# A selective state-space scan: reading the states under C by turning them, instead of multiplying by broadcast rows

## The reference, cut to what matters

```python
x_dbl = einsum('bld,ed->ble', x, Wx)           # dt_rank 64 | B 16 | C 16
dt = softplus(x_dbl[..., :64] @ Wdt.T + bdt)
dA  = exp(dt[..., None] * A)                   # A = -exp(A_log), 512 x 16
dBx = (dt * x)[..., None] * Bm[:, :, None, :]
def step(hc, inp):                             # over the tokens of a sequence
    hc = dA_t * hc + dBx_t
    return hc, einsum('bdn,bn->bd', hc, C_t)
y = ys + x * Dp
y = y * silu(z)
out = einsum('bld,ed->ble', y, W_out)
```

## Time and profile before

| | before |
|---|---|
| median of 3 runs | 4064.31 us |
| profiled execution | 4061.75 us |
| its span, first to last instruction | 4059.8 us |
| mean granted TensorE clock over the span | 0.932 |
| DVE busy / PE busy / ACT busy / POOL busy | 2756.5 / 3550.4 / 1951.2 / 1562.0 us |

### The profile page before, as it was taken

The page is one execution under the profiler, slowest core; times in us unless marked ns, Lnnn a source line. Parts: engine busy times, 40 slices in busy tenths (PEclk is TensorE's granted clock), DMA queues, the critical chain, the costliest instruction groups (busy, mean ns, idle before and its releaser), DMA issues. The chain is left out here.

```text
span 4059.8 us, 128360 instructions
## 1 busy us (share of the span) xinstructions
PE 3550.4 (87%) x53914; PEld 2521.8 (62%) x53915; DVE 2756.5 (68%) x4627; ACT 1951.2 (48%) x3015; POOL 1562.0 (38%) x1491
## 2 busy tenths in 40 slices
PE   6999999999783699669999999998788888877778
PEld 4888888888672466448888888885233333333357
DVE  5777777777543122257777777776799999999964
ACT  2666666666441122126666666664444444444432
POOL 3333333333132100233333333330088777778800
PEclk8999999999895899869999999998898989999889
DMA  2010010000006100110100010000132222222200
GB/s 67 28 36 28 28 34 29 28 28 20 10 1 244 46 31 31 49 56 28 36 28 28 30 33 28 28 20 25 24 81 71 72 70 68 70 72 81 72 25 21
DMA packets 79948, 182.69 MB, mean 45 GB/s; under 512 B 10754, under 2 KB 31266, under 8 KB 79042
## 3 DMA queue, kind: packets, MB, share of 16 engines
q1 hardware_dynamic: 76354, 166.57, 13.2%
q0 software_dynamic: 3072, 8.39, 0.6%
HBM read 157.36 MB, written 17.56 MB: 43 GB/s over the span
## 5 line engine op out<-in xcount | busy, mean ns | idle before, releaser
L654 ACT ACTIVATE x_probs<-x_score_ps 128x1024 f32<-128x1024 f32 (+1 forms) x896 | 814.2, 960 | 708.2 <-PE x_score_ps L563 701.9
L714 DVE TENSOR_REDUCE x_maxes<-x_misc_ps 128x1 f32<-128x512 f32 (+1 forms) x1792 | 1020.9, 625 | 31.0 <-PE x_misc_ps L481 25.6
L678 POOL CAST x_kT_hi<-x_kT 128x512 fp32r<-128x512 f32 (+1 forms) x448 | 256.3, 572 | 1286.5 <-ACT x_kT L627 1063.1
L1742 PE MATMUL b_acc_ps<-b_read,ident 128*128 128x512 f32 x1024 | 571.1, 689 | 183.5 <-POOL b_read L1828 150.3
L1820 POOL TENSOR_TENSOR b_drive<-b_b_all,b_dtx 128x1024 f32<-128x1024 f32 x256 | 602.6, 2355 | 332.8 <-DVE b_dtx L1900 282.0
L1862 DVE TENSOR_TENSOR_SCAN b_state<-b_decay_ps,b_drive 128x512 f32<-128x512 f32 x512 | 607.0, 1205 | 12.5 <-POOL b_drive L1820 12.5
L557 PE MATMUL x_score_ps<-x_qz,x_kT 32*128 32x128 f32 x13312 | 591.2, 277 | 1.4 <-issue 1.2
L1810 ACT ACTIVATE b_decay_ps<-b_dt,b_a_neg 128x504 f32<-128x504 f32 x512 | 350.0, 685 | 462.3 <-DVE b_state L1862 462.3
L1742 PEld LDWEIGHTS b_acc_ps<-b_read,ident 128*128 128x128 f32 x1024 | 196.1, 213 | 503.8 <-POOL b_read L1828 251.1
L557 PEld LDWEIGHTS x_score_ps<-x_qz,x_kT 32*128 32x128 f32 x13312 | 501.4, 182 | 4.5 <-issue 2.5
L531 PE MATMUL x_misc_ps<-x_probs,x_v 128*32 128x64 f32 x26624 | 464.5, 221 | 0.0
(11 more groups left out here) (283 smaller groups left out, 5607.9 us busy)
## 6 DMA issues: line engine op xcount, KB each, us to landing
x_raw<-in_ctxT SPq DMA_DIRECT2D x64, 800.5 KB, 4.5
b_b_all<-b_bc_rows SPq DMA_DIRECT2D x128, 256.0 KB, 3.6
b_c_all<-b_bc_rows SPq DMA_DIRECT2D x128, 256.0 KB, 3.1
m_w<-in_m_w SPq DMA_DIRECT2D x16, 704.0 KB, 19.3
m_w<-in_m_w SPq DMA_DIRECT2D x8, 768.0 KB, 20.3
m_slot_rows<-m_zero SPq DMA_DIRECT2D x1, 4992.0 KB, 17.2
m_block_rows<-m_slot_rows SPq DMA_DIRECT2D x39, 128.0 KB, 2.0
m_slot_out<-m_out SPq DMA_DIRECT2D x39, 128.0 KB, 1.7
```

The lines of the kernel that those rows point to most:

```text
L654: nc.scalar.activation(probs[rows, s % 2, js, 0:n], score_ps[rows, js, 0:n], ACT.Exp).then_inc(exp_done, 1)
L678: nc.gpsimd.tensor_copy(kT_hi[:, at % 3, 0:m * even].rearrange("p (c k) -> p c k", c=m)[:, :, 0:kn], kT[:, b % 2, c:c + m, k0:k0 + kn]).th ...
L714: nc.vector.tensor_reduce(maxes[:, c:c + m, j, k0 // NB], bank(op)[:, 0:m * even].rearrange("p (c k) -> p c k", c=m)[:, :, 0:kn], AX.X, AL ...
L1742: nc.tensor.matmul(acc_ps[:, c, :], ident[:, :], read[:, c, :], start=False, stop=True, skip_group_check=True).then_inc(acc_done, 1)
```

## The change

The broadcast of C over the partitions is gone, and so are the three VectorE reads and the GpSimd read of a state. Instead the state is turned so that tokens lie on the partitions, where C_n(token) is a single number for each partition. There are TPB = 4 token tiles of 128 in a block. For every state TensorE transposes each token tile (four 128 x 128 transposes, one for each channel chunk) into one of two PSUM banks. ScalarE copies token tiles 0 to 2 out with C as its per-partition scale, and TensorE turns these back and adds them to acc_ps with four products per tile, in which the copied tile is the weights and the identity is what is streamed. Token tile 3 is summed over the 16 states in turned form by VectorE (`sum_tile`), and is turned back once, at the end of the pass. State and drive get two buffers. C itself is turned once, at the start of the first pass. In `project` the high and low parts, their buffers and their DMAs go. VectorE waits for the last gather of the whole pass before it takes the first chunk of acc_ps.

```diff
-                    sp.dma_start(bc_rows[d, :, tokens], xdbl[R:, d, tokens]).then_inc(rows_out, 16)
-                    for i, part in enumerate((hi, lo)):
-                        sp.dma_start(c_rows[d, i, :, tokens], part[R + NS:, d, :].bitcast(F32)).then_inc(rows_out, 16)
-                    sp.wait_ge(rows_out, blk * (2 * 48) + (d + 1) * 48)
-                    sp.sem_inc(rows_free, 1)
+                    sp.dma_start(b_rows[d, :, tokens], xdbl[R:R + NS, d, tokens]).then_inc(rows_out, 16)
+            sp.wait_ge(rows_out, NBLK * 2 * 16)
...
-                    nc.scalar.activation(xdbl[:, d, ds(blk * NB, NB)], dbl_ps[:, d, :], ACT.Copy)
-                    act.wait_ge(rows_free, blk * 2 + d + 1)
-                    nc.scalar.activation(hi[R:, d, :], dbl_ps[R:, d, :], ACT.Copy).then_inc(hi_done, 1)
+                    nc.scalar.activation(xdbl[:, d, ds(blk * NB, NB)], dbl_ps[:, d, :], ACT.Copy).then_inc(rows_done, 1)
...
-                low_parts(blk - 1)
-            low_parts(NBLK - 1)
...
+    BY_ACT = TPB - 1
+    PARTS = NS * BY_ACT + 1
+    drive = sb("b_drive", [P, 2, CI, NB])
+    state = sb("b_state", [P, 2, CI, NB])
+    read = sb("b_read", [P, BY_ACT, DI])
+    total = sb("b_total", [P, DI])
...
 @block.tensor
+        def turn_rows():                       # after the first Wdt products, pass 0 only
+            own = slice(R, R + 2 * NS)
+            for d in range(2):
+                for t in range(NT):
+                    ins = nc.tensor.transpose(turn_ps[:, d, t * 2 * NS:(t + 1) * 2 * NS], xdbl[own, d, t * P:(t + 1) * P],
+                                              ident[own, own])
+            ins.then_inc(rows_turned, 1)
+        def turn(k, i):
+            if i == 0:
+                pe.wait_ge(state_done, (k + 1) * CI)
+            if i >= 2:
+                pe.wait_ge(read_done, k * BY_ACT + i - 1)
+            elif k > 0 and i == 0:
+                pe.wait_ge(read_done, k * BY_ACT)
+            elif k > 0:
+                pe.wait_ge(total_done, k)
+            for c in range(CI):
+                ins = nc.tensor.transpose(turn_ps[:, i % 2, c * P:(c + 1) * P], state[:, k % 2, c, i * P:(i + 1) * P],
+                                          ident[:, :])
+            ins.then_inc(turn_done, 1)
+        def add_up(i, part):
+            for c in range(CI):
+                ins = nc.tensor.matmul(acc_ps[:, c, i * P:(i + 1) * P], part[:, c * P:(c + 1) * P], ident[:, :],
+                                       start=False, stop=True, skip_group_check=True)
+            ins.then_inc(acc_done, 1)
+        def gather(k, i):
+            pe.wait_ge(read_done, k * BY_ACT + i + 1)
+            add_up(i, read[:, i, :])
...
-                if n < NS - 1:
-                    make_c(k + 1)
-                for c in range(CI):
-                    gather(k, c)
+                turn(k, 0)
+                turn(k, 1)
+                if n > 0:
+                    gather(k - 1, 2)
+                turn(k, 2)
+                gather(k, 0)
+                turn(k, 3)
+                gather(k, 1)
+            gather((p + 1) * NS - 1, 2)
+            pe.wait_ge(total_done, (p + 1) * NS)
+            add_up(BY_ACT, total)
...
 @block.scalar
+        def read_tile(p, n, i):
+            k = p * NS + n
+            act.wait_ge(turn_done, k * TPB + i + 1)
+            if k > 0:
+                act.wait_ge(acc_done, p * PARTS + (n - 1) * BY_ACT + i + 1 if n > 0 else p * PARTS)
+            nc.scalar.activation(read[:, i, :], turn_ps[:, i % 2, :], ACT.Copy, scale=c_of(p, n, i)).then_inc(read_done, 1)
...
             for n in range(NS):
                 for c in range(CI):
+                    make_decay(p, n, c)
+                    if n > 0 and c > 0:
+                        read_tile(p, n - 1, c - 1)
+            for i in range(BY_ACT):
+                read_tile(p, NS - 1, i)
...
 @block.gpsimd
-            if k > 0:
-                pool.wait_ge(state_done, (k - 1) * CI + c + 2)
+            if k > 1:
+                pool.wait_ge(state_done, (k - 2) * CI + c + 2)
-                if n > 0:
-                    read_last(k - 1)
-            read_last(p * NS + NS - 1)
...
 @block.vector
+        def sum_tile(p, n):
+            dve.wait_ge(turn_done, (k + 1) * TPB)
+            if n == 0:
+                ins = nc.vector.tensor_scalar(total[:, :], tile, c_of(p, n, BY_ACT), None, ALU.mult)
+            else:
+                ins = nc.vector.scalar_tensor_tensor(total[:, :], tile, c_of(p, n, BY_ACT), total[:, :], ALU.mult, ALU.add)
+            ins.then_inc(total_done, 1)
...
             for n in range(NS):
                 for c in range(CI):
-                    if c < CI - 1:
-                        scan(p, n, c + 1)
-                    elif n < NS - 1:
-                        scan(p, n + 1, 0)
-                    if c < VE:
-                        read_chunk(p, n, c)
+                    if c == CI - 1 and n > 0:
+                        sum_tile(p, n - 1)
+                    scan(p, n, c)
+            sum_tile(p, NS - 1)
+            dve.wait_ge(acc_done, (p + 1) * PARTS)
             for c in range(CI):
-                dve.wait_ge(acc_done, ((p + 1) * NS - 1) * CI + c + 1)
                 nc.vector.tensor_tensor(xc[:, d, c, tokens(p)], acc_ps[:, c, :], zs[:, c, tokens(p)], ALU.mult
                                         ).then_inc(y_done, 1)
```

More of the change, by code:

```diff
@@ L1663, in recur @@
     b_all = sb("b_b_all", [P, 2, NB])
-    c_all = sb("b_c_all", [P, 2, NB])
-    c_row = sb("b_c_row", [1, 2, 2, NB], F32R)
-    drive = sb("b_drive", [P, CI, NB])
-    state = sb("b_state", [P, CI, NB])
-    read = sb("b_read", [P, CI, NB])
+    c_turned = sb("b_c_turned", [P, 2, NT, NS])
+    drive = sb("b_drive", [P, 2, CI, NB])
+    state = sb("b_state", [P, 2, CI, NB])
+    read = sb("b_read", [P, BY_ACT, DI])
+    total = sb("b_total", [P, DI])
     acc_ps = ps("b_acc_ps", [P, CI, NB])
-    c_ps = ps("b_c_ps", [P, 2, NB])
+    turn_ps = ps("b_turn_ps", [P, 2, NB])
     decay_ps = ps("b_decay_ps", [P, 2, NB])
@@ L1674, in recur @@
     b_in = [sem(f"b_b_in{j}") for j in range(2)]
-    c_all_in = [sem(f"b_c_all_in{j}") for j in range(2)]
-    c_in = [sem(f"b_c_in{j}") for j in range(2)]
     step_done = sem("b_step_done")
@@ L1781, in _, with make_decay @@
     def _(act):
+        def make_decay(p, n, c):
+            q = (p * NS + n) * CI + c
+            if n == 0:
+                act.wait_ge(dt_done, p * CI + c + 1)
+            if q >= 2:
+                act.wait_ge(state_done, q - 1)
+            nc.scalar.activation(by_sequence(decay_ps[:, c % 2, :])[:, :, inside(p)],
+                                 by_sequence(dt[:, c, :])[:, :, inside(p)], ACT.Exp,
+                                 scale=a_neg[:, direction(p)[0], c, n:n + 1]).then_inc(decay_done, 1)
+        def read_tile(p, n, i):
[4 more added lines that the diff above has]
+            nc.scalar.activation(read[:, i, :], turn_ps[:, i % 2, :], ACT.Copy, scale=c_of(p, n, i)).then_inc(read_done, 1)
         nc.scalar.activation(a_neg[:, :, :, :], a_log[:, :, :, :], ACT.Exp).then_inc(a_done, 1)
@@ L1802, in _ @@
             act.wait_ge(edge_done, d + 1)
+            if p == 0:
+                act.wait_ge(rows_turned, 1)
+                nc.scalar.activation(c_turned[:, :, :, :],
+                                     turn_ps[:, :, :].rearrange("p d (t r) -> p d t r", r=2 * NS)[:, :, :, NS:], ACT.Copy
+                                     ).then_inc(c_done, 1)
+                act.wait_ge(c_done, 1)
             for n in range(NS):
+                k = p * NS + n
                 for c in range(CI):
-                    q = (p * NS + n) * CI + c
-                    if n == 0:
-                        act.wait_ge(dt_done, p * CI + c + 1)
-                    if q >= 2:
-                        act.wait_ge(state_done, q - 1)
-                    nc.scalar.activation(by_sequence(decay_ps[:, c % 2, :])[:, :, inside(p)],
-                                         by_sequence(dt[:, c, :])[:, :, inside(p)], ACT.Exp,
-                                         scale=a_neg[:, d, c, n:n + 1]).then_inc(decay_done, 1)
+                    make_decay(p, n, c)
[3 more added lines that the diff above has]
+                read_tile(p, NS - 1, i)
     @block.gpsimd
```

105 lines of the change are left out of this document (35 added, 70 removed).

## The result

| | before | after |
|---|---|---|
| median of the runs | 4063.06 us (4061.2 to 4066.16, 4 runs) | 4039.52 us (4030.61 to 4040.71, 4 runs) |
| profiled execution | 4061.75 us | 4039.19 us |
| Mamba block in it, layer norm to layer norm | 1082.1 us | 1058.2 us |

The ratio after to before is 0.9937, with the interval [0.9919, 0.9954]: faster by 0.63%, a small gain that stands clear of the noise, and 2.5 us from the 4042 that was predicted. The profiled executions differ by 22.6 us: the Mamba block took 23.9 us less, the other layers 1.3 us more.

A forecast was written before the change was run, and what follows sets the result against it. DVE's four scans and three reads bound each state at 6.25 us. Passes -60, pass ends +38.5, projection -5, clock falls +5 gave -21.5 from 4061.75, so 4040; runs' median 2.6 higher, said as 4042; range 3995 to 4090.

The forecast's parts named there:

- The state: One state of the recurrence: the time between successive states' fourth scans falls from 6.25 to 5.72 us.
- Rival 4: In a state, DVE's own work is the bound after all: 5.17 us, 62 us less, 3980; chance 0.12.
- Rival 2: Handovers between engines cost more than counted: 6.0 us a state, 31 us in all, 4073; chance 0.16.
- The pass: 16 states, first scan to last scan's end: 99.5 us before, 92.0 after; 60 us less in eight passes.
- the first ring: A pass's first fourth scan to its second: 5.38 us at full clock, plus 1.9 us for half clock.
- the ring: In a state, PE, ACT and DVE wait on each other in turn, DVE before `sum_tile`: 5.72 us a state.
- Between the passes: From a pass's last scan to the next first scan: 4.7 us more, seven times, 33 us.
- few more falls of the clock: An allowance in the total for further drops of PE's clock: +5 us.
- The end of the last pass: `output` waits for chunk 3, ready 9.0 us after the scan's end instead of 3.4: 5.6 us more.
- The projection: Before the recurrence: without low parts ahead of convolutions and with an earlier last DMA, 5 us less.
- Does the clock hold?: PE's clock in the recurrence: 1.00 expected except at a pass's start; 0.91 or lower over the stage would refute.
- Rivals 1 and 3: PE's clock in the recurrence: 1, low as before, 4081, chance 0.17; 3, transposes don't hold it, 4176, chance 0.05.

The follow-up runs named there:

- late_sum: Changed kernel with VectorE's sum of token tile 3 moved behind the next state's fourth scan; 3956.02 us, ratio 0.9743 to the kernel before.
- warm_start: Changed kernel plus 52 unneeded identity transposes (20 in the first pass) on TensorE before each pass's first state; 4024.8 us, ratio 0.9909 to the kernel before.
- gather_early: Changed kernel with TensorE adding tile 2 before the next state's turns instead of between them; 3995.61 us, ratio 0.9839 to the kernel before.
- chunk_wait: Changed kernel with VectorE taking each chunk at a pass's end after that chunk's own last product; 4031.21 us, ratio 0.9919 to the kernel before.
- four_by_act: Changed kernel with ScalarE reading all four token tiles, TensorE summing and turning them back, VectorE summing nothing; 3987.44 us, ratio 0.9822 to the kernel before.
- all_four: Changed kernel with the edits of late_sum, gather_early, warm_start and chunk_wait together; 3938.33 us, ratio 0.9702 to the kernel before.
- project_back: Changed kernel with the old projection's high and low parts and DMAs made again, read by nobody; 4041.32 us, ratio 0.9958 to the kernel before.

## Why the prediction was right, point by point

**The state.** Predicted 5.72 us, measured 5.72 to 5.73 in all 112 steps behind the first ring of a pass. The steps hold one by one. Counted from the end of the fourth scan (3086.85 in the timeline above): ACT on tile 0 at 0.76 (predicted 0.76), tile 2's transposes at 1.89 (1.88), tile 0's products at 2.32 (2.32), tile 3's transposes at 3.22 (3.20), the sum at 3.86 (3.84). DVE's idle time is 0.50 us where I had 0.45. Rival 4, DVE's own work at 5.17 us, did not hold for the change, and late_sum shows that it was one slot in the queue away: 5.12 us. Rival 2, dearer handovers, fell with the same number.

**The pass.** Predicted 92.0 us, measured 91.5 to 92.4: 735.5 us for eight against 796.8 before, 61.3 us less where I had 60. Inside it the price of the clock at the start was about right: the first ring took 6.65 to 7.53 us, 7.1 on average, against 5.38 + 1.9 = 7.3. warm_start confirms both parts, since with the clock held the ring is 5.38.

**Between the passes.** Predicted 23.3 us. Three of seven were 23.32; four were 24.24 to 24.55. These four are most of the "few more falls of the clock", for which I had 5 us. No row stood behind that term. The falls came to 3.5 us more than before at the boundaries and about 1.5 at the end of the last pass, 5 in all, and that this met the guess is luck. Windows of a short boundary (first row) and of a long one show it; the second row starts at the long one's first chunk, and the third is the same part as the first, 4.4 us behind the first chunk:

```profile
3149.30:3156.30 7.00, 7.00 (x33) 6.19 (x33) 3.56 (x6) 6.84 (x11) 0.00 (x0) 1.00 0.00 0
...
3260.60:3265.00 4.40, 3.65 (x8) 1.56 (x8) 3.99 (x6) 2.06 (x3) 0.00 (x0) 0.88 0.00 0
3265.00:3272.00 7.00, 7.00 (x19) 4.98 (x18) 2.68 (x4) 5.95 (x10) 0.00 (x0) 0.58 0.00 0
```

The timeline of the long one has the price. PE's eight products with Wdt, which stand on the path, take 4.63 us instead of the 3.70 of the short boundary:

```profile
3261.35 4.63 PE L1757 MATMUL b_acc_ps<-b_xdbl,b_wdt 64*128 64x512 f32 x8 [0.78 <-DVE b_xc L1937]
```

Together the boundaries cost 36.4 us more than before, against 33 + 5 predicted for boundaries and falls. What set off the fall at four of seven boundaries was not tried, and stays open. It varies with edits elsewhere: three of seven boundaries were long in late_sum, one in warm_start, and none in gather_early, chunk_wait, four_by_act and all_four.

**The end of the last pass** cost 7.2 us where I had 5.6: from the last scan's end to the next layer's first operation, 21.0 us against 13.8. Up to the end of chunk 3 it is 5.7, as counted from the earlier trace rows. The other 1.5 are the clock again: it was at 0.50 from 3844.2 to 3847.6, and PE, idle for 2.58 us before them, took 8.86 us for the 32 products with W_out. At a short boundary, and at the same place in the kernel before, they take 7.17:

```profile
3843.73 8.86 PE L1747 MATMUL b_turn_ps<-b_wout,b_xc 128*128 128x256 f32 x32 [2.58 <-DVE b_xc L1937]
```

**The projection** gained 6.2 us in this pair of traces where I had 5. The stretch varies by 1.8 us among the eight kernels with the new projection (134.1 to 135.9), so the gain over the kernel before is 4.4 to 6.2 us; project_back, which puts only the old work back, shows 2.6 to 4.4.

**The sum.** -61.3 + 36.4 + 7.2 - 6.2 = -23.9 us, the block's difference; predicted -60 + 33 + 5.6 + 5 - 5 = -21.5 (33 + 5.6 stood as 38.5). The four terms, with the falls counted to the boundaries, were off by -1.3, -1.6, +1.6 and -1.2 us. So part of the closeness of the total is that one miss took back another, and the 1.3 us more of the other layers took back half of the rest.

**Does the clock hold?** Yes, and better than before: 0.96 over the stage. Half clock took 75 us there instead of 162, all of it at boundaries and the starts of passes. Rivals 1 and 3 fell with that: PE kept 1.00 through states in which 16 of the 40 records are transposes.

**One number was wrong.** I said that DVE's busy time would go down by 165 us; it went down by 136. The bracket behind the number gives 128 x (3 x 0.66 - 0.74) = 159 us, not 165. Summed instruction by instruction, DVE's time did fall by 166 us (3004.6 to 2839.0), with the low parts of the projection in it. But the page counts time in which two instructions overlap only once, and of that there was 248 us before and 219 after. Nothing in the forecast hung on it.

**Why a lean ring gave so little.** VectorE's own work for a state went down from 6.25 to 5.12 us (late_sum), and 0.61 of that 1.13 us came back in the ring: 0.50 as idle time before the sum, and the rest mainly because a sum that had to wait no longer overlaps the end of the scan before it (0.08 us in late_sum). Of the 61.3 us that the passes gained, 43.6 went back where the pipeline drains: the last state's ring lies open at each of eight ends, with 3.85 us of waiting before the last sum (112 x 0.50 + 8 x 3.85 = 87, the idle time of the group). With the sum one slot later and the three other edits, the same design reaches 3938.33 us.

## What to carry to other kernels

When a step is handed around several engines with in-order queues, write the ring's timetable from one event and look for the instruction that waits in it, and then for what stands behind that instruction in its own queue. If nothing needs its result soon, put it one slot later: here that was worth some 80 us, more than three times the whole change. And count what a deeper pipeline adds where it drains and refills; here that took back 43.6 of 61.3 us.

## What the runs showed of the hardware

- TensorE's granted clock was held at 1.00 through 3.4 us of nothing but fp32 transposes (warm_start, 3163.00 to 3166.40), and the transposes of the pass's first state then took 1.09 us for eight instead of 1.94.
- The copy by ScalarE with a per-partition scale out of PSUM, 128 x 512, took 0.68 us, inside the 0.60 to 0.69 of the earlier trace rows. VectorE's multiply-add from PSUM took 0.75 us, just over the 0.74 that I had as its upper end, and 0.72 where it followed a scan directly (late_sum).
- Turning a tile back by a product whose weights are the data and whose streamed operand is the identity ran at 0.11 us for each record of 128 columns (eight in 1.06 us with the last one's 0.28), the same as the transposes. With nothing else to wait for, 544 such records and transposes filled 60 us of PE (four_by_act, 3060 to 3120).
